# Row numbers copied a span ahead on GpSimd, and no wait for landed rows inside a chunk, in a three-layer graph kernel

## What is computed

```python
xn = layernorm(x)
h = xn
for l in range(3):                       # the three graph layers
    agg = segment_sum(h[src], edge_type * 3125 + dst, 8 * 3125)
    h = act(einsum('rnd,rde->ne', agg.reshape(8, 3125, 256), W[l]) + h @ root[l] + bias[l])
x = x + h + linear_attention(xn)         # act: relu, relu, sigmoid
x = x + mixture_of_experts(layernorm(x)) # 8 experts, the best 2 for each node
```

## Time and profile before

| | us |
|---|---|
| median of 3 runs | 3850.56 (3849.05 to 3857.96) |
| span of the profiled execution | 4114.6 |
| PE busy in it | 3088.8 (75%) |
| POOL busy in it | 2472.2 (60%) |
| DVE, ACT busy in it | 1180.3, 400.3 |
| first gather to last gather | 28.5 to 3863 |

### The profile page before, as it was taken

How to read it: one execution, slowest core, us unless ns; L and a number is a source line. 1 busy time by engine, 2 the same in 40 slices (tenths; PEclk the granted TensorE clock), 3 DMA queues, 4 the chain that set the end, 5 groups by cost and what they waited for, 6 DMA issues and landing times. The chain is left out here.

```text
span 4114.6 us, 51204 instructions
## 1 busy us (share of the span) xinstructions
PE 3088.8 (75%) x16304; PEld 2668.8 (65%) x16304; DVE 1180.3 (29%) x2874; ACT 400.3 (10%) x1010; POOL 2472.2 (60%) x2784
## 2 busy tenths in 40 slices
PE   3677677777787777878777777677877777877885
PEld 3566566666676666656666656566677767766775
DVE  4222222222223322222122222333333333333323
ACT  1000000000000000000000000001112112211232
POOL 5666666666666666666666656665555555555233
PEclk8778787777778777677777677878888888898898
DMA  6333333433344333333333333334455455455675
GB/s 167 116 114 117 114 119 114 126 116 114 117 118 130 92 90 93 92 94 90 92 93 92 92 105 91 90 92 135 150 164 162 151 158 172 148 161 162 205 249 200
DMA packets 276975, 524.33 MB, mean 127 GB/s; under 512 B 60783, under 2 KB 180331, under 8 KB 276716
## 3 DMA queue, kind: packets, MB, share of 16 engines
q0 software_dynamic: 121152, 331.40, 27.6%
q1 hardware_dynamic: 154396, 190.17, 14.6%
q10 hardware_dynamic: 1296, 1.24, 0.1%
HBM read 458.71 MB, written 63.91 MB: 127 GB/s over the span
## 5 line engine op out<-in xcount | busy, mean ns | idle before, releaser
L703 POOL DMA_INDIRECT arena<-rows_dram,arena x2396 | 2275.6, 950 | 1157.0 <-issue 705.7
L1888 PE MATMUL bank<-arena 128*128 128x128 f32 x4836 | 1084.4, 335 | 485.5 <-DMA arena<-rows_dram,arena 240.8
L1888 PEld LDWEIGHTS bank<-arena 128*128 128x128 f32 x4836 | 888.0, 232 | 665.5 <-issue 330.2
L1487 DVE TENSOR_TENSOR arena<-arena,bank 128x256 f32 x807 | 338.2, 419 | 2433.4 <-remote 1401.9
L1892 PE MATMUL bank<-arena 128*128 128x128 f32 x4836 | 901.9, 324 | 152.1 <-issue 145.4
L1892 PEld LDWEIGHTS bank<-arena 128*128 128x128 f32 x4836 | 792.0, 235 | 185.7 <-issue 184.5
L1748 PE MATMUL bank<-arena 128*128 128x256 f32 x2400 | 657.3, 411 | 95.5 <-issue 52.2
L1748 PEld LDWEIGHTS bank<-arena 128*128 128x128 f32 x2400 | 466.6, 208 | 177.8 <-issue 125.6
L1406 DVE TENSOR_TENSOR arena<-bank,arena 128x1408 f32<-128x1408 f32 x222 | 355.3, 1603 | 11.6 <-issue 11.6
L1802 PE MATMUL bank<-arena 128*128 128x128 f32 x1152 | 172.8, 307 | 68.1 <-DVE arena L1335 38.3
L1802 PEld LDWEIGHTS bank<-arena 128*128 128x128 f32 x1152 | 162.0, 220 | 76.0 <-issue 74.9
(11 more groups left out here) (227 smaller groups left out, 1533.1 us busy)
## 6 DMA issues: line engine op xcount, KB each, us to landing
arena<-in_L_ffn_W_dram SPq DMA_DIRECT2D x112, 512.0 KB
arena<-in_L_ffn_W_dram SPq DMA_DIRECT2D x44, 1024.0 KB
arena<-rows_dram,arena POOLq DMA_INDIRECT x2418
xs_dram<-zslot SPq DMA_DIRECT2D x25, 1224.0 KB
arena<-xs_dram SPq DMA_DIRECT2D x56, 136.0 KB
rows_dram<-arena SPq DMA_DIRECT2D x50, 128.0 KB
arena<-in_L_gnn_weights_dram SPq DMA_DIRECT2D x6, 1024.0 KB
arena<-ys_dram SPq DMA_DIRECT2D x8, 640.0 KB, 8.1
```

The source lines that it names most:

```text
L703: nc.gpsimd.indirect_dma_start(out=gath[:, slot, :], out_offset=None, in_=rows_dram[l], in_offset=bass.IndirectOffsetOnAxis(ap=idx_ring[:, ...
L1487: nc.vector.tensor_tensor(acc, acc, edge_sum(l, q).rearrange("p (k r n) -> p k r n", k=KD, r=REL), ALU.add).then_inc(S["tile_add"], 1)
L1888: nc.tensor.matmul(edge_sum(l, q)[:, 0:WC], gath[:, slot, 0:P], onehot[:, slot, :], start=first, stop=last)
```

## The change

`idx_ring` becomes twice as long, two halves of one span each. At chunk 1 of a span GpSimd copies all 33 row numbers of the *next* span into the other half (`next_rows`), with a new semaphore `ring_made`. The gathers of a span read its own half. The wait for `group_mm` at the head of each chunk stays, with the same values; the wait for the copy stands at chunk 0 alone, and for a copy that was issued about two chunks earlier. `REST_AFTER` is empty, so the wait for landed rows behind the fifth gather is gone. The first two spans of layer 0 are copied by ScalarE (one more copy, 128x44). To keep to the number of semaphores `agg_clean` is folded into `const`. In the last span of layer 2, VectorE's early step waits for `ring_made` in place of the last `ix_ready`. What is computed is the same. The diff, cut to its core:

```diff
-REST_AFTER = (4,)
+REST_AFTER = ()
...
-        idx_ring = carve(SLOTS_G).bitcast(I32)
+        idx_ring = carve(2 * SLOTS_G).bitcast(I32)
...
-                    def ring(s, a, n):
-
-                        used = -(-CH * (a + 1) // GT)
+                    def freed(s, a):
+
                         if is_first(s):
-                            freed = GROUPS * (l - 1) + (SG * (NSPAN - 1) - (-CH // GT) if a == 0 else GROUPS) if l > 0 else 0
-                        else:
-                            freed = GROUPS * l + SG * (s.m - 1) + (CH * (a + 2)) // GT
-                        wait(pool, "group_mm", freed)
-                        if l > 0 and is_first(s) and a == CPS - 1:
-                            wait(pool, "miss_mm", l)
-                        part = idx_part if l > 0 and is_first(s) and a == 0 else idx_i[:, bass.ds(CH * (CPS * s.m + a), n)]
-                        nc.gpsimd.tensor_copy(idx_ring[:, CH * a:CH * a + n], part).then_inc(S["ix_ready"], 1)
+                            return GROUPS * (l - 1) + (SG * (NSPAN - 1) - (-CH // GT) if a == 0 else GROUPS) if l > 0 else 0
+                        return GROUPS * l + SG * (s.m - 1) + (CH * (a + 2)) // GT
+
+                    def next_rows(s):
+
+                        o = ring_half(l, 1 - s.par)
+                        if not is_last(s):
+                            if l > 0 or not is_first(s):
+                                nc.gpsimd.tensor_copy(o, idx_i[:, bass.ds(SPAN * (s.m + 1), SPAN)]).then_inc(S["ring_made"], 1)
+                        elif not final:
+                            nc.gpsimd.tensor_copy(o[:, 0:CH], idx_part).then_inc(S["ring_made"], 1)
+                            nc.gpsimd.tensor_copy(o[:, CH:SPAN], idx_i[:, CH:SPAN]).then_inc(S["ring_made"], 1)
...
                         for a, n in chunks_of(s):
...
-                            ring(s, a, n)
+                            wait_apart(pool, "group_mm", freed(s, a))
+                            if a == 1:
+                                next_rows(s)
...
-                            wait(pool, "ix_ready", CHUNKS * l + CPS * s.m + a + 1)
-                            pool.nop(nofuse=True)
+                            if a == 0 or l == 0 and is_first(s):
+                                wait_apart(pool, "ring_made", rings(l, s))
                             for j in range(n):
-                                gather(CH * a + j)
+                                gather(CH * a + j, at)
                                 if j in REST_AFTER:
                                     wait_apart(pool, s_gath[CH * a + j - 1], gathered(l, CH * a + j - 1, s.m))
```

More of the change, by code:

```diff
@@ L36 @@
 SLOTS_G = CPS * CH
+RINGS = NSPAN + 1
 GT = 3
@@ L328, in gps_layer @@
         names = """src_in edge_in wrel_in mixw_in ffw_in win_moved out_st
-            const pads ids first_st agg_clean src_made edges_made edge_turned edge_back viol_sum flag_set
+            const pads ids first_st src_made edges_made edge_turned edge_back viol_sum flag_set
             var_made sd_made nm_made xn_made xa_made
-            ix_ready hot_ready tile_mm group_mm tile_add folded node_ready stage_full agg_zero node_mm hn_made
+            ix_ready ring_made hot_ready tile_mm group_mm tile_add folded node_ready stage_full agg_zero node_mm hn_made
             rows_st last_st miss_mm miss_out hn_turned hT_made
@@ L462, in gathered, with ring_half, rings @@
             return ((NSPAN if slot < LAST_SPAN else NSPAN - 1) * l + m + 1) * 16
+        def ring_half(l, par):
+            h = (par + l) % 2
+            return idx_ring[:, SPAN * h:SPAN * (h + 1)]
+        def rings(l, s):
+            return 1 if l == 0 and is_first(s) else RINGS * l + s.m
         def place_of(t, par):
@@ L687, in _ @@
                                     pattern=[[-1, P]], channel_multiplier=1).then_inc(S["const"], 1)
-            nc.gpsimd.memset(agg_w, 0.0).then_inc(S["agg_clean"], 1)
+            nc.gpsimd.memset(agg_w, 0.0).then_inc(S["const"], 1)
             pool.wait_ge(S["src_in"], 3 * 16)
@@ L701, in _, with gather @@
             for l in range(LAYERS):
-                def gather(slot):
+                def gather(slot, at):
                     nc.gpsimd.indirect_dma_start(
                         out=gath[:, slot, :], out_offset=None, in_=rows_dram[l],
-                        in_offset=bass.IndirectOffsetOnAxis(ap=idx_ring[:, slot:slot + 1], axis=0)).then_inc(s_gath[slot], 16)
+                        in_offset=bass.IndirectOffsetOnAxis(ap=at[:, slot:slot + 1], axis=0)).then_inc(s_gath[slot], 16)
                 def scatter(t, b):
@@ L739, in span @@
                                 continue
-                            ring(s, a, n)
+                            wait_apart(pool, "group_mm", freed(s, a))
+                            if a == 1:
+                                next_rows(s)
                             if l > 0 and is_first(s) and a == 1:
-                                wait(pool, "last_st", 16 * l)
-                            wait(pool, "ix_ready", CHUNKS * l + CPS * s.m + a + 1)
-                            pool.nop(nofuse=True)
+                                wait_apart(pool, "last_st", 16 * l)
+                            if l > 0 and is_first(s) and a == CPS - 1:
+                                wait_apart(pool, "miss_mm", l)
+                            if a == 0 or l == 0 and is_first(s):
+                                wait_apart(pool, "ring_made", rings(l, s))
                             for j in range(n):
-                                gather(CH * a + j)
+                                gather(CH * a + j, at)
                                 if j in REST_AFTER:
@@ L764, in chunk @@
                         for j in range(n):
-                            gather(CH * h + j)
+                            gather(CH * h + j, idx_ring)
                     def general(t, p0):
@@ L852, in _ @@
                 nc.scalar.copy(idx_ring[:, CH * a:CH * (a + 1)], idx_i[:, CH * a:CH * (a + 1)]).then_inc(S["ix_ready"], 1)
+            nc.scalar.copy(idx_ring[:, CH * AHEAD:2 * SPAN], idx_i[:, CH * AHEAD:2 * SPAN]).then_inc(S["ring_made"], 1)
             act.wait_ge(S["edges_made"], 1)
@@ L966, in _ @@
             act.wait_ge(S["first_st"], 16 * (NG + LAYERS - 1))
-            act.wait_ge(S["agg_clean"], 1)
+            act.wait_ge(S["const"], 10)
             for l in range(LAYERS):
@@ L1391, in _ @@
             dve.wait_ge(S["flag_set"], 1)
-            dve.wait_ge(S["agg_clean"], 1)
+            dve.wait_ge(S["const"], 10)
             dve.wait_ge(S["win_moved"], 32)
@@ L1446, in beside @@
                                 if q == LAST_FREE:
-                                    dve.wait_ge(S["ix_ready"], CHUNKS * LAYERS)
+                                    dve.wait_ge(S["ring_made"], RINGS * LAYERS - 2)
                                     nc.vector.memset(zsig[:, 0:1], 0.0).then_inc(S["low_free"], 1)
```

1 line of the change is left out of this document (added).

## The result

| | us |
|---|---|
| before, median in the same comparison | 3852.57 (3849.05 to 3857.96) |
| after, median of 4 runs | 3406.49 (3404.83 to 3419.39) |
| ratio | 0.8852, 95% interval 0.8835 to 0.887 |
| span of the profiled execution of after | 3401.5 |

The change takes 446 us off, 11.5%.

What follows compares the result with a forecast made beforehand. GpSimd's stream of gathers was taken to bound nearly all three layers, with TensorE following. Stage gains of 130 + 127 + 40 + 60 = 357 us, taken as 350, gave 3500 us; range 3420 to 3760 us.

Steps and rivals of the forecast that it cites:

- GpSimd's stream is the bound, and what is taken from it comes off the time: In nearly all of the three layers GpSimd's gathers bound the time; its stream gets shorter by 463 us.
- A waited copy 0.65 us, a new one 0.25: GpSimd's row-number copies: 220 waited ones cost 143 us, 73 new unwaited ones 18 us, at most 47.
- Met waits 0: On GpSimd, waits on `group_mm` and `ring_made` met long before cost 0, with 90 us kept for the range.
- The stalls of 263 us: GpSimd's 263.3 us idle ahead of its copies, waiting for TensorE, was claimed absent from unprofiled runs.
- cost for each record: Profiling was said to slow TensorE per instruction record; TensorE has 32608 of the 51204 records.
- the floor of 834 us: TensorE's busy time in layer 2 with experts, taken as the length at which it takes over as bound.
- Layers 0, 1 and 2 without experts, 130, 127 and 40 us: Gains forecast for the first three stages, from GpSimd's shorter stream, with TensorE's limit also weighed in layer 1.
- the lower of its two bounds: Layer 1's gain of 121 us, from TensorE busy 924 plus some 100 us of waits for rows, 1024 us.
- Layer 2 with experts, 60 us: In the expert stage GpSimd's stream falls to 765 us but TensorE takes over; gain 25 to 91, taken as 60.
- The clock: TensorE falling behind GpSimd would run dense and get the upper clock level, against a loss of the gain.
- The shared port: VectorE's 1.76 us accumulator clearing showed no block of GpSimd's gathers, so the sum has nothing for it.
- the gap of 264 us: Profiled span of the kernel before, 4114.6 us, against the runs' median, 3850.56; expected to widen after the change.

Runs made afterwards that it cites:

- second profile of before: The unchanged kernel before the change, profiled once more: 3851.86 us, with a profiled span of 3849.7 us.
- the rests on old rows: Kernel before the change, each rest kept but waiting for rows asked for four gathers earlier instead of one: 3564.85 us, ratio 0.9238.

## Why the prediction was off, point by point

**GpSimd's stream is the bound, and what is taken from it comes off the time: right.** The rests came to 293 us alone. The prediction had 338 for them (481 less the copies' 143), since it had counted the idle at layer borders and other small waits with them: in the second profile of before these are 1143.0 - 719 - 99 - 289 = 36 us. The copies' gain went the other way, 125 us in the sum and 153 on top of the missing rests. Only 17 us of error are left of 45 and 28.

**A waited copy 0.65 us, a new one 0.25: right and too high.** The new one costs 0.08, so 18 us in the sum should have been 6.

**Met waits 0: right**, as far as the rests on old rows can tell: 4.8 us for 220 by the medians, none by the ratios.

**The stalls of 263 us are not in the runs: right; because each record costs TensorE time: wrong.** The "cost for each record" was never priced. And PE's busy time was read as an effect of profiling for the stalls, and in the next step, from the same execution, as a hard fact for the floor of 834 us.

**Layers 0, 1 and 2 without experts, 130, 127 and 40 us: right**, 131, 127 and 40. The match to a microsecond is partly luck, since the rests were put too high and the copies' gain too low. And in layer 1 the lower of its two bounds, a TensorE that can't go under 924 + 100 = 1024 us, had the same fault as the next step, with the 100 taken from waits in the disturbed profile. The stage took 1024.0 us in after, but not because of TensorE: with 88 more passes in each span it took 10 us more.

**Layer 2 with experts, 60 us: this step failed.** "PE is busy 834. Here TensorE takes over" held the stage at 834 to 902 us. It took 752, and the gain was 148. Three things were wrong in it. The 834 came from a disturbed execution; an undisturbed one has 763. Those 763 were at a granted clock of 0.90, and the work is some 650 to 670 us at 0.99. And in the same prediction the paragraph on the clock had said that a TensorE that runs dense gets the upper level, but the sum by stages did not use it. GpSimd's own bound for that stage was worked out as 765 us, 13 off; taken alone it gives 160 us of gain there, 457 in all and about 3394 us.

**The clock: right.** It rose from 0.796 over the whole of the second profile of before to 0.862. The loss that the paragraph feared from the lower level did not come. The rule of the Trainium skill ("TensorE: Matmul & The Clock Gate", Part 1) that sustained activity releases the clock is borne out, by the 0.99 of the runs with more passes.

**The shared port: right.** The clearing of the accumulator and the gathers beside it, in after:

```profile
641.96 1.76 DVE L1408 MEMSET arena<- 128x2048 f32 x1 [0.38 <-issue]
```

```profile
641.54 0.94 POOL L715 DMA_INDIRECT arena<-rows_dram,arena  x1 [0.30 <-issue]
642.79 0.95 POOL L715 DMA_INDIRECT arena<-rows_dram,arena  x1 [0.30 <-issue]
644.04 0.95 POOL L715 DMA_INDIRECT arena<-rows_dram,arena  x1 [0.30 <-issue]
```

They keep 0.95 and 1.25 us with the rests gone. Of the block for which "SBUF — State Buffer" of the Trainium skill gives the reason, nothing shows for this instruction. The page itself ("Who interferes with whom") says that what contends is VectorE in a two-port mode or with two inputs in SBUF, and it does not list this clearing among the instructions that can enter such a mode; the trace agrees, with 0.95 us for the gather that started at 642.79, inside the clearing.

**What was to be seen in the profile after.** Gathers 1.25 us apart without a break but the copy: so it is. Stalls for `group_mm` to grow and the gap of 264 us to widen: neither, the profiled span is 3401.5 and the runs 3406.49. The wait for TensorE as GpSimd's largest idle in the expert stage: no, it is 5.5 us. The text had also said "If they fall by over 430, TensorE was never near"; they fell by 446. Layers 0 and 1 took 11 us more of TensorE's work in each of their spans of 41 for 6 and 10 us in all; the expert stage had room for 5 or 6 us in a span.

**The range.** It ended at 3420, though the case in which the whole stream's gain arrives was worked out there as 3388 and tied to a rise of the clock, for which the prediction's own paragraph on the clock had argued. The sum's own bound was left outside with a chance of 0.02; taken into the range it would have held the time.

## What to carry to other kernels

When you ask which engine is next, do not take TensorE's busy time at a granted clock below 1 as the length it can't go under: give its passes the duration that a dense stretch of the same profile shows, and compare that with the other engine's stream. A wait costs by the age of what it waits for: put it where it is long met and it costs next to nothing, put it behind work of a microsecond ago and the engine stands for the whole of that work's latency. And where a profiled span is far from the median of the runs, profile again before explaining the difference; no number from such an execution should stand for a floor.

## What the runs showed of the hardware

- A gather of 128 rows takes GpSimd 0.95 us and the next starts 0.30 us later, whether its rows have 512 bytes or 1 KB, and whether the rows of the one before have landed or not: 33 in a row keep 1.25 us. What the 0.30 us are is open.
- A copy of 128x33 on GpSimd fits into those 0.30 us but for 0.08, as long as nothing waits for it; the wait makes it 0.67.
- More matmuls can make TensorE's busy time shorter: in layer 1 932 us at a clock of 0.74, 866 at 0.80, and 838 at 0.99 with 1074 records more.
- Still open: what disturbed the first profile of before, why the rests wait 33 us longer once the copies are ahead, and whether a gather of fewer rows takes GpSimd less.
